# GpSimd's scale of the first norm moved behind the key remainder, ScalarE's context rounding ahead of the second exponentials

## What is computed

```python
x = x + tanh(g_xattn[0]) * xattn(layernorm(x), ctx_1024, ctx_1024, wq, wk, wv, wo_w, wo_b)
x = x + tanh(g_ffn[0])   * ffn(layernorm(x), w_router, w_fc, w_gate, w_proj)
```

## Time and profile before

| | us |
|---|---|
| three runs | 1833.91, 1836.87, 1838.42 (median 1836.87) |
| profiled execution | 1835.99, span 1834.2 |
| TensorE busy | 1520.0 (83% of the span) |
| VectorE busy | 1410.9 (77%) |
| ScalarE busy | 1133.7 (62%) |
| GpSimd busy | 1088.1 (59%) |

### The profile page before, as it was taken

One profiled execution on the slowest core, in us unless ns is written; L12 is line 12 of the kernel. 1 busy time (PEld: TensorE's weight loads), 2 busy tenths in 40 slices (PEclk: granted clock), 3 DMA queues, 4 the chain that ended last, 5 costly groups with the idle time before them and its releaser, 6 DMA issues. The chain is left out here.

```text
span 1834.2 us, 50716 instructions
## 1 busy us (share of the span) xinstructions
PE 1520.0 (83%) x16843; PEld 1222.3 (67%) x16844; DVE 1410.9 (77%) x2993; ACT 1133.7 (62%) x2321; POOL 1088.1 (59%) x1490
## 2 busy tenths in 40 slices
PE   4888889988899898898988989986169888898871
PEld 3666666666666666666666666664059888898871
DVE  3777787777877777777777777775968999999964
ACT  3667667677666766766766767674236555565540
POOL 3455465555655555555555555551826888788866
PEclk9999999999999999999999999997569999999995
DMA  2112122121221211212212122242026888898876
GB/s 90 48 58 86 57 71 72 57 86 57 69 74 57 85 58 57 86 57 73 70 57 86 57 70 73 70 145 81 6 72 198 260 263 261 262 286 269 263 228 207
DMA packets 156096, 210.21 MB, mean 115 GB/s; under 512 B 18688, under 2 KB 104832, under 8 KB 156032
## 3 DMA queue, kind: packets, MB, share of 16 engines
q1 hardware_dynamic: 125312, 142.36, 24.5%
q0 software_dynamic: 12288, 33.57, 6.4%
q10 hardware_dynamic: 18432, 33.56, 5.1%
HBM read 125.54 MB, written 83.89 MB: 114 GB/s over the span
## 5 line engine op out<-in xcount | busy, mean ns | idle before, releaser
L505 DVE TRANSPOSE_TENSOR_REDUCE part_max<-ST 128x16 f32<-128x512 f32 x512 | 321.3, 685 | 171.9 <-PE ST L684 168.4
L360 ACT ACTIVATE probs_t<-ST 128x512 f32<-128x512 f32 x512 | 262.5, 596 | 68.2 <-PE ST L699 68.2
L711 PE MATMUL PO<-probs_t,v_aug 128*32 128x128 f32 x4096 | 205.2, 298 | 108.6 <-ACT probs_t L360 95.0
L288 POOL TENSOR_TENSOR ct_lo<-c_in_sb,ct_hi 128x512 fp32r<-128x512 f32 x64 | 82.4, 1288 | 278.0 <-ACT ct_hi L378 278.0
L711 PEld LDWEIGHTS PO<-probs_t,v_aug 128*32 128x32 f32 x4096 | 94.4, 114 | 204.5 <-ACT probs_t L360 192.6
L437 ACT ACTIVATE xn<-x_in_sb,off,rstd 128x256 f32<-128x256 f32 x128 | 70.0, 594 | 224.7 <-POOL off L284 224.7
L1190 ACT ACTIVATE x_hi<-scaled 128x256 fp32r<-128x256 f32 x128 | 53.5, 418 | 210.9 <-DMA scaled<-xn_d 131.9
L1259 PE MATMUL GU<-we_hi,s_hi 128*128 128x256 f32 x512 | 155.8, 304 | 0.0
L1153 POOL DMA_INDIRECT first<-eo_d,collect_row x128 | 126.0, 984 | 44.4 <-issue 24.0
L316 POOL TENSOR_TENSOR q_rest<-q_rot,q_head 128x512 f32<-128x512 f32 x64 | 82.4, 1288 | 112.7 <-ACT q_head L413 112.7
L1153 POOL DMA_INDIRECT second<-eo_d,collect_row x128 | 122.6, 958 | 42.3 <-issue 38.7
(11 more groups left out here) (158 smaller groups left out, 5565.7 us busy)
## 6 DMA issues: line engine op xcount, KB each, us to landing
eo_d<-eo ACTq DMA_DIRECT2D x128, 256.0 KB
x_in_sb<-x SPq DMA_DIRECT2D x64, 256.0 KB, 2.8
c_in_sb<-ctx_t SPq DMA_DIRECT2D x64, 256.0 KB, 2.8
xr_sb<-x SPq DMA_DIRECT2D x64, 256.0 KB, 4.0
x_d<-x SPq DMA_DIRECT2D x64, 256.0 KB, 4.1
xn_d<-xn SPq DMA_DIRECT2D x64, 256.0 KB, 4.2
scaled<-xn_d SPq DMA_DIRECT2D x128, 128.0 KB
scaled<-x_d SPq DMA_DIRECT2D x128, 128.0 KB
```

The costliest lines, as they stand in the source:

```text
L288: pool.tensor_tensor(ct_lo[:].rearrange("p k b t -> p (k b t)"), c_in_sb[:, n.par].rearrange("p k b t -> p (k b t)"), ct_hi[:].rearrange(" ...
L360: act.activation(probs_t[:, b, i].rearrange("p j q -> p (j q)"), ST[i][:], ACT.Exp) \
L505: dve.tensor_reduce(part_max[:, i, 0], ST[i][:].rearrange("p (c l) -> p c l", l=32), AX_X, ALU.max, apply_transpose=True).then_inc(M["part ...
L711: last = pe.matmul(PO[32 * j:32 * j + 32, i * SEQ:(i + 1) * SEQ], v_aug[:, n.par, b, head], probs_t[:, b, i, j], start=True, stop=True)
```

## The change

GpSimd: `scale_of_norm` leaves the head of the step, where it was done for pair s + 2, and stands behind `key_rest(s + 1)` and ahead of `context_rest(s + 2)`, for pair s + 3. So the scale of a pair is worked out one step earlier, in the same step in which VectorE writes its `mv`. ScalarE: `context_head(s + 2)` moves from behind the second sequence's four exponentials to ahead of them.

```diff
@@ GpSimd
         def step(s):
             if (s - 2).real:
                 scale_of_norm2(s - 2)
-            if (s + 2).real:
-                scale_of_norm(s + 2)
             if (s - 1).real:
                 residual(s - 1)
             if (s + 1).real:
                 ...
                 key_rest(s + 1)
+            if (s + 3).real:
+                scale_of_norm(s + 3)
             if (s + 2).real:
                 context_rest(s + 2)
@@ ScalarE
             if (s + 1).real:
                 masked_rests(s + 1)
+            if (s + 2).real:
+                context_head(s + 2)
             if s.real:
                 for i in range(4):
                     exp_unit(s, 1, i)
             if (s + 2).real:
-                context_head(s + 2)
                 input_head(s + 2)
```

## The result

The changed kernel takes 1759.67 us (median of 4 runs, 1754.3 to 1760.7) against 1835.39 (4 runs); the ratio is 0.958, with a 95% interval of 0.9555 to 0.9604. The forecast was 1762, the range 1752 to 1796.

What follows compares the result with a forecast made beforehand. TensorE was taken as nearest to the bound, waiting on ScalarE's late exponential. 61 steps x (0.70 wait + 0.55 clock) = 76.3, less 1.1 at the start, gives 75 us: 1836.9 - 75 = 1762, range 1752 to 1796.

Steps and rivals of the forecast that it cites:

- The bound: Attention loop: TensorE nearest to the bound, idle 1.34 us before the first context product because `off` reaches ScalarE late.
- the sum: Whole kernel: 61 steps x (0.70 + 0.55) = 76.3, less 1.1 once, gives 75 us less.
- The wait, 0.70 us a step: First half of a step: ScalarE's exponential starts 0.60 or 0.79 us sooner, mean 0.70, shortening TensorE's wait; bounds 0 and 0.78.
- The clock, 0.55 us a step: TensorE in the loop: clock falls, three in eight steps, all vanish with the shorter wait, saving 0.55 us a step.
- Rival A: Attention loop: the wait shortens but the clock falls as often; 42 us gained, 1795 us; chance 0.10.
- C: Attention loop: the shorter step falls in line with the clock and is hit every time; slower, 1851 us; chance 0.04.
- `ct_hi`'s cover: ScalarE ahead of the second exponentials: 0.80 us free hides `ct_hi`'s 0.65, with 0.15 us to spare.
- The start, +1.1 us: First steps: `ct_lo` of pair 0 stands behind pair 1's scale, delaying TensorE's first projection; +1.1 us once, bounds 0 and 1.5.
- GpSimd's idle time: Sign of being right: `ct_lo` hardly waits behind `off`, and GpSimd's idle time moves to the second norm's `mv`.

Runs made afterwards that it cites:

- the last try: Changed kernel with the transposes of `att` put into TensorE's remaining 0.77 us wait and the maxima turned sooner; 1777.16 us, ratio 0.9659.
- the filled wait: Kernel before with eight spare TensorE products in the wait ahead of the first context products; 1797.96 us, ratio 0.9787.
- late-exponential kernel: Changed kernel with a spare ScalarE copy of 640 columns ahead of the first sequence's exponentials; 1823.61 us, ratio 0.9928.
- the second copy: Changed kernel with a spare ScalarE copy of the same 512 columns ahead of `ct_hi`; 1771.16 us, ratio 0.9628.

## Why the prediction was right

*The bound.* The place was right: TensorE's wait ahead of the first context products, made by ScalarE's order, made by the late `off`. The gain is in the steps that have this wait. They are steps 2 to 61, 60 of them; step 1, which the sum counted too, waits 0.75 us in the kernel before already.

*The wait, 0.70 us a step.* Measured 1.35 to 0.77 and 1.54 to 0.77, 0.67 on the mean; 17.97 us a step where 17.95 was forecast. Step 62 of the kernel before had shown the value beforehand. The forecast had `at_hi` and the maximum's products allow the exponentials at the same moment. It is the products that set it: the exponentials start at 725.27, 0.63 us behind L700 (forecast 0.62), while `at_hi`, begun at 724.71, would have let them start 0.08 earlier by the forecast's 0.48. In the last try, where `at_hi` no longer stands ahead of them, they start 0.62 us behind the same products:

```profile
715.94 2.07 ACT L360 ACTIVATE probs_t<-ST 128x512 f32<-128x512 f32 x4 [3.41 <-PE ST L702]
```

*The clock, 0.55 us a step.* Forecast to go entirely, and it did, 35.6 us by the filled wait against 34. The forecast took three falls in eight steps from one stretch; the whole trace has 24 in 60, 7 of them behind the shorter kind of wait and 17 behind the longer. That they would all go, it argued only from the steps with and without a fall, and in that it had some luck: with a wait of 1.33 us in every step they come back, at 1.06 they do not, and no row of before showed where between 0.77 and 1.34 us the limit lies. The filled waits, in the kernel before and in the late-exponential kernel, show the cause: same step, same order, work in the wait, no falls. Rival A is refuted, and with it the rule of the Trainium skill ("TensorE: Matmul & The Clock Gate", section "HAM oscillation — how this bites in real kernels") by which these falls would have had another cause and stayed: in this kernel they came behind waits of 1.3 to 1.6 us and went with them. C is refuted too. But the late-exponential run shows that A had a true part: with one length of wait the number of falls is not fixed.

*The parts.* This is where the forecast read the rows least well. It told the two moves as one gain, and did not ask what each would do alone. Each brings it all. The rows of before held this already: `xn` and what follows it had to start sooner by no more than the gain itself, 0.60 or 0.79 us. ScalarE's move alone took 1.28 us off the wait for `off` (3.60 to 2.32), GpSimd's took all of it.

*`ct_hi`'s cover.* Hidden, as said; 0.15 us was forecast as the least that would be left, 0.28 to 0.31 is there, and the second copy cost time once it was used up.

*The start, +1.1 us.* It came, and was given back. The first key projection starts at 22.60 us instead of 21.61, having waited 1.79 us for `ct_lo` instead of 0.78, and the first scores come 1.19 us later, at 34.62 instead of 33.43. But the first context products come at 42.41 instead of 42.62. In between TensorE does the same projections in both kernels without a wait, and the clock rises 2 us earlier in the changed one, as the stretch from 38 to 39 us shows, first before, then after (columns as in the earlier trace rows):

```profile
38.00:39.00 1.00, 1.00 (x7) 1.00 (x6) 0.00 (x0) 0.00 (x0) 0.00 (x0) 0.50 0.11 8
```

```profile
38.00:39.00 1.00, 1.00 (x10) 1.00 (x10) 1.00 (x2) 0.00 (x0) 0.00 (x0) 1.00 0.88 281
```

By step 1 the changed kernel is 0.20 us behind (61.33 against 61.13). So the term was right for its wait; that the clock gave it back no one forecast, and why the clock rose when it did is open. It is about half of the difference between the 75 us forecast and the 76.8 of the profiled executions; by the medians the gain is 75.7.

*GpSimd's idle time* was to move to the second norm's `mv`. 1.3 us a step did; most went to the rotation, 4.30 us ahead of `k_rot` in the rows shown, and the length of the step shows no cost of it.

## What to carry to other kernels

When an engine in the middle holds the bound engine up, work out how much earlier its input must come before counting moves: two edits that both bring it early enough bring the gain once, and the simpler one will do. A wait of the engine that sets the pace, if that is TensorE, can cost twice, once for itself and once for the clock behind it; filling it with spare products parts the two in one run, and is worth trying where the wait can't be removed. Work that fills one engine's wait for another is nearly free only there; moved out of it, most of it is paid, here 0.39 us a step for transposes that take about 0.6.

## What the runs showed of the hardware

In the kernel before and the late-exponential one TensorE's clock falls to 1.2 GHz behind waits of 1.3 to 1.6 us, in 24 of 60 steps of the one and in 17 of the other, and each fall costs about 1.5 us here. A stretch inside the fall that follows 752.85:

```profile
754.00:756.00 2.00, 2.00 (x24) 1.26 (x24) 0.23 (x1) 0.25 (x1) 1.41 (x2) 0.50 0.89 307
```

Waits of 0.77 and 1.06 us, in every step of the loop, brought none. At 1.33 us the same kernel had the granted clock at 0.99 up to 640 us and 0.96 behind it, with the same order and the same wait in both. Eight products of 256 columns, some 1.2 us of work, in the wait kept the clock at 1.00 in both kernels in which they were tried.
